# Every embedding gather of a one-core DLRM tower waits for the gather two before it

## What is computed

```python
s = jnp.sum(x, axis=-1)                        # x: (2048, 39, 64), the picked rows
z = s[:, _ROW] * s[:, _COL]                    # all pairs, (2048, 741)
h = jnp.concatenate([z, dense_ctx], axis=1)    # (2048, 757)
h = jnp.maximum(h @ W_top1 + b_top1, 0.0)      # 512 columns
h = jnp.maximum(h @ W_top2 + b_top2, 0.0)      # 256 columns
y = h @ W_top3                                 # 1 column
```

## Time and profile before

| | |
|---|---|
| median of 3 runs | 319.54 us (318.14 to 319.74) |
| profiled execution: span, first to last instruction | 314.8 us |
| PE (matmul) busy | 207.8 us, 66% |
| DVE (VectorE) busy | 144.2 us, 46% |
| ACT (ScalarE) busy | 81.2 us, 26% |
| POOL (GpSimd) busy | 114.8 us, 36% |
| the chain that ended last: PE, "issue" | 51%, 31% |

### The profile page before, as it was taken

The page is one execution under the profiler, slowest core; times in us unless marked ns, Lnnn a source line. Parts: engine busy times, 40 slices in busy tenths (PEclk is TensorE's granted clock), DMA queues, the critical chain, the costliest instruction groups (busy, mean ns, idle before and its releaser), DMA issues.

```text
span 314.8 us, 4373 instructions
## 1 busy us (share of the span) xinstructions
PE 207.8 (66%) x1659; PEld 126.9 (40%) x1659; DVE 144.2 (46%) x384; ACT 81.2 (26%) x144; POOL 114.8 (36%) x124
## 2 busy tenths in 40 slices
PE   0652102499794321118956988856999999999996
PEld 0310000344131100004613655653566776667784
DVE  2000000157990000002964679561589988968440
ACT  0200010268980000000064224210132424035432
POOL 6777777000077777740473320537310000000000
PEclk9955555589667555555985999977599999999999
DMA  7811131189924132115693676999124029100000
GB/s 290 286 29 30 27 93 25 46 300 413 418 87 129 25 69 89 25 21 186 221 342 121 217 254 218 350 351 244 25 60 150 2 77 275 52 2 2 2 0 0
DMA packets 13557, 43.70 MB, mean 139 GB/s; under 512 B 3216, under 2 KB 4256, under 8 KB 13408
## 3 DMA queue, kind: packets, MB, share of 16 engines
q1 hardware_dynamic: 9392, 39.42, 36.1%
q0 software_dynamic: 3712, 3.81, 5.8%
q10 hardware_dynamic: 432, 0.19, 0.2%
HBM read 43.14 MB, written 0.27 MB: 138 GB/s over the span
## 4 chain that ended last, share of the span: by engine, by line
PE 51%; issue 31%; DVE 7%; ACT 5%; another core or an unknown queue 3%; DMA 2%; ACTq 0%; DVEq 0%
PE g L1119 8%; PE ph L1226 8%; PE ph L1227 7%; PE ph L1230 6%; PE ph L1119 5%; PE s L1205 3%; DVE mid_sums L505 2%; PE g L1165 2%; PE g L1102 2%; PE ph L1246 2%; PE g L1140 2%; DMA stage<-early 2%; PE ph L1250 2%; PE ph L1247 2%
## 5 line engine op out<-in xcount | busy, mean ns | idle before, releaser
L429 POOL DMA_INDIRECT rows<-tab,idc x68 | 65.8, 968 | 77.9 <-DVE w_lo L522 32.8
L438 POOL DMA_INDIRECT rows<-tab,idc x48 | 46.4, 968 | 36.7 <-DVE bsum L587 18.4
L1119 PE MATMUL g<-stage,fc 128*32 128x100 f32 x378 | 27.3, 318 | 41.2 <-issue 40.2
L1119 PE MATMUL ph<-stage,fc 128*32 128x96 f32 (+2 forms) x378 | 20.9, 285 | 39.9 <-issue 30.6
L1226 PE MATMUL ph<-z_hi,w_hi 126*128 126x512 f32 (+1 forms) x96 | 44.8, 467 | 0.0
L536 DVE TENSOR_SCALAR hots<-hots,fc 125x2048 bf16<-125x2048 bf16 x28 | 20.7, 751 | 43.6 <-issue 42.5
L1227 PE MATMUL ph<-z_hi,w_lo 126*128 126x512 f32 (+1 forms) x96 | 39.7, 413 | 0.7 <-issue 0.7
L1230 PE MATMUL ph<-z_lo,w_hi 126*128 126x512 f32 (+1 forms) x96 | 39.3, 409 | 0.0
L1119 PEld LDWEIGHTS g<-stage,fc 128*32 128x32 f32 x378 | 15.8, 139 | 52.6 <-issue 50.9
L1119 PEld LDWEIGHTS ph<-stage,fc 128*32 128x32 f32 x378 | 12.4, 134 | 49.1 <-issue 47.9
L478 DVE CAST mparts<-g 125x100 bf16<-125x100 f32 x3 | 0.8, 262 | 62.4 <-PE g L1119 50.4
(11 more groups left out here) (88 smaller groups left out, 269.0 us busy)
## 6 DMA issues: line engine op xcount, KB each, us to landing
stage<-middle SPq DMA_DIRECT2D x17, 800.0 KB
hots<-shelf_scratch SPq DMA_DIRECT2D x17, 512.0 KB
stage<-early SPq DMA_DIRECT2D x3, 768.0 KB
stage<-middle SPq DMA_DIRECT2D x3, 750.0 KB
stage<-early SPq DMA_DIRECT2D x3, 640.0 KB
rows<-tab,idc POOLq DMA_INDIRECT x116
slot_b<-slot_scratch SPq DMA_DIRECT2D x8, 224.0 KB
stage<-early SPq DMA_DIRECT2D x3, 512.0 KB
```

Source lines behind the costliest of these rows:

```text
L429: pool.indirect_dma_start(rows[:, n % ROW_RING, i, :], None, gathered[i], bass.IndirectOffsetOnAxis(ap=idc[:, n, i:i + 1], axis=0)).then_i ...
L438: pool.indirect_dma_start(rows[:, n % ROW_RING, i, :], None, gathered[i], bass.IndirectOffsetOnAxis(ap=idc[:, n, i:i + 1], axis=0)).then_i ...
L1119: mm = pe.matmul(bank[j * LANE:(j + 1) * LANE, 0:w], band, stage[:, q, (r * 4 + j) * w:(r * 4 + j + 1) * w], start=(x == 0), stop=(x == PA ...
```

## The change

Two semaphores per ring slot and group take the place of one. The j-th gather of a tile signals number j mod 2. Before a gather is issued, GpSimd waits until the last gather but one has landed: in the same tile through the count of that semaphore, for the first two gathers of a tile through the tile (or group) ahead of it. So at most two gathers are on the way at any time. The order of the gathers, their number and size stay. VectorE's sums wait for both semaphores of their tile. There are 114 added waits on GpSimd, one in front of every gather but the first two.

```diff
-        rows_a_in = [sem(f"rows_a_in{t}") for t in range(ROW_RING)]
-        rows_b_in = [sem(f"rows_b_in{t}") for t in range(ROW_RING)]
+        rows_a_in = [[sem(f"rows_a_in{t}_{x}") for x in range(2)] for t in range(ROW_RING)]
+        rows_b_in = [[sem(f"rows_b_in{t}_{x}") for x in range(2)] for t in range(ROW_RING)]
...
+        def rows_a(c, x):
+            return 16 * sum((NA - SUMMED[k] + 1 - x) // 2 for k in range(c % 2, c + 1, 2))
...
+            def group_ahead_landed(c, t, kind, j):
+                n = c * TILES + t
+                if t:
+                    of, n = kind, n - 1
+                elif kind == "b":
+                    of, n = "a", n + TILES - 1
+                else:
+                    of, c, n = "b", c - 1, n - 1
+                slot = n % ROW_RING
+                if of == "a":
+                    x = (NA - SUMMED[c] - 2 + j) % 2
+                    pool.wait_ge(rows_a_in[slot][x], rows_a(c, x))
+                else:
+                    x = (NB - 2 + j) % 2
+                    pool.wait_ge(rows_b_in[slot][x], rows_b(c, x))
...
-                for i in range(SUMMED[c], NA):
-                    pool.indirect_dma_start(rows[:, n % ROW_RING, i, :], None, gathered[i],
+                for j in range(NA - SUMMED[c]):
+                    i = SUMMED[c] + j
+                    if j >= 2:
+                        pool.wait_ge(rows_a_in[slot][j % 2], rows_a(c - 2, j % 2) + 16 * (j // 2))
+                    elif n:
+                        group_ahead_landed(c, t, "a", j)
+                    pool.indirect_dma_start(rows[:, slot, i, :], None, gathered[i],
                                             bass.IndirectOffsetOnAxis(ap=idc[:, n, i:i + 1], axis=0)
-                                            ).then_inc(rows_a_in[n % ROW_RING], 16)
+                                            ).then_inc(rows_a_in[slot][j % 2], 16)
...
-                dve.wait_ge(rows_a_in[slot], rows_a(c))
+                for x in range(2):
+                    dve.wait_ge(rows_a_in[slot][x], rows_a(c, x))
```

More of the change, by code:

```diff
@@ L263, in mid_loads, with rows_b @@
             return 16 * sum(1 + (SUMMED[x] > 4) for x in range(2, c + 1))
[L265 to L269, removed]
+        def rows_a(c, x):
+            return 16 * sum((NA - SUMMED[k] + 1 - x) // 2 for k in range(c % 2, c + 1, 2))
+        def rows_b(c, x):
+            return 16 * ((NB + 1 - x) // 2) * (c // 2 + 1)
         def selects(c, which):
@@ L427, in fetch_a @@
                     pool.wait_ge(a_summed, n - ROW_RING + 1)
-                for i in range(SUMMED[c], NA):
-                    pool.indirect_dma_start(rows[:, n % ROW_RING, i, :], None, gathered[i],
+                for j in range(NA - SUMMED[c]):
[5 more added lines that the diff above has]
+                    pool.indirect_dma_start(rows[:, slot, i, :], None, gathered[i],
                                             bass.IndirectOffsetOnAxis(ap=idc[:, n, i:i + 1], axis=0)
-                                            ).then_inc(rows_a_in[n % ROW_RING], 16)
+                                            ).then_inc(rows_a_in[slot][j % 2], 16)
             def fetch_b(c, t):
                 n = c * TILES + t
+                slot = n % ROW_RING
                 if c >= 2:
                     pool.wait_ge(b_summed, n - ROW_RING + 1)
-                for i in range(NA, NL):
-                    pool.indirect_dma_start(rows[:, n % ROW_RING, i, :], None, gathered[i],
+                for j in range(NB):
+                    i = NA + j
+                    if j >= 2:
+                        pool.wait_ge(rows_b_in[slot][j % 2], rows_b(c - 2, j % 2) + 16 * (j // 2))
+                    else:
+                        group_ahead_landed(c, t, "b", j)
+                    pool.indirect_dma_start(rows[:, slot, i, :], None, gathered[i],
                                             bass.IndirectOffsetOnAxis(ap=idc[:, n, i:i + 1], axis=0)
-                                            ).then_inc(rows_b_in[n % ROW_RING], 16)
+                                            ).then_inc(rows_b_in[slot][j % 2], 16)
             pool.memset(tparts[:, :, :], 0.0)
@@ L585, in sum_b @@
                 slot = (c * TILES + t) % ROW_RING
-                dve.wait_ge(rows_b_in[slot], rows_b(c))
+                for x in range(2):
+                    dve.wait_ge(rows_b_in[slot][x], rows_b(c, x))
                 dve.tensor_reduce(bsum[:, t, 0:NB], rows[:, slot, NA:, :], AX.X, ALU.add).then_inc(b_summed, 1)
```

## The result

| | before | after |
|---|---|---|
| median of 3 runs each | 319.54 us (318.14 to 319.74) | 270.79 us (270.01 to 272.56) |
| span of the profiled execution | 314.8 us | 269.0 us |
| last gather starts at, and from there to the end | 228.91, 85.9 us | 243.59, 25.4 us |

The change made the kernel faster: ratio 0.850, 95% interval 0.845 to 0.854. I had forecast 325 us. The direction was wrong; the time lies where rival 1 put it.

What follows compares the result with a forecast made beforehand. TensorE standing during gather runs (94 of 314.8 us), then matmuls in the last stretch, bound the kernel. 5.6 + 2.5 - 2.5 + 0.4 = 6.0 us more, later runs 0: span 320.8, plus 4.7, predicted 325 us; range 319 to 347.

Steps and rivals of the forecast that it cites:

- rival 1: Slower gathers end TensorE's standing and then bound the kernel: 262 us, 237 to 314, chance 0.38.
- main step: Waits are already met in mid run, so gathers stay 1.25 us apart and TensorE's slow pace inside runs stays.
- The wait in mid run: GpSimd's wait without loads: landing 2.14 us against a look at 2.2 us, so met and free; far end 6 us per run.
- The stall: TensorE nearly stands during long gather runs and a few us behind: two slow stretches, 94 of 314.8 us, taken to stay.
- a tenth less pace is enough: Argument for rival 1: leftover about 0.11 us per gather, 9% of the 1.25 us pace, so slightly slower gathers free TensorE.
- picture of a pile that forms: Rival 1's mechanism: 40 gathers pile something up; if landing signals queue behind it, the new wait keeps it from forming.
- Delay beside loads: Gathers wait beside table loads: third gather 3.0 us late; 5.6 us in the first run, 2.5 us in the second.
- Rows are needed late: Later gather runs: last sum comes 61 us behind the last gather's start, so their 5 to 20 us delay counted 0.
- Rival 1's sum: Gather-bound time: 116 gathers at 1.3 us, 151; 36 beside loads, 54 more; 4 start, 25 end, 5 around: 239 us.
- rival 1's signs: "Issue" below 15% of the chain, first slow stretch's 30 matmuls done by 25 us, GpSimd busy nearly to the end.
- Rivals 2 and 3: 2: waits met, delay given back, 319.5 us, chance 0.16. 3: late landing signals lengthen TensorE's standing, 340 us, chance 0.06.
- the slow case: The outcome that the change makes the kernel slower, chance 0.43; the forecast's own range was 0 to 28 us more.

Runs made afterwards that it cites:

- the copy with the stall: The kernel before, unchanged, run and traced again on another chip: 318.12 us against 318.32, ratio 0.996; 17% "issue" in its chain.
- the bound of three: At most three gathers on the way, added to the kernel before: 235.76 us, ratio 1.191, measured only without the stall.
- the slower memset: A GpSimd memset of 128x512 in front of each gather of the kernel before, no landing waits: 235.51 us, ratio 1.195, without the stall.
- at most 4: Kernel before with at most four gathers on the way: 299.49 us (ratio 0.950) with the stall, 213.10 us (1.077) without.
- memset 256: Kernel before with a 128x256 GpSimd memset before each gather, no landing waits: 276.91 us against 317.43 with the stall; 214.79 us (1.086) without.

## Why the prediction was wrong

**The step that failed** is the one the forecast rested on, "whether waiting gathers still make TensorE stand". I took it that they do, because I held that in mid run the wait is already met and the pace stays. I had written: "I am wrong in the main step if TensorE's pace inside a run of gathers changes". It did, from 30 matmuls to 287 in 39 us. The measured time lies within the 236 to 338 us that I gave over all cases only because that range takes in rival 1; the forecast's own 319 to 347 us misses it, and that the wide range holds is no merit of the forecast.

**The wait in mid run.** I set the landing (2.14 us, from the packets of the earlier trace rows) against the time at which GpSimd looks (2.2 us) and called the wait met. The packets are not the signal. Without loads beside it, the profile gives 2.5 us from issue to landing, and the trace after has a gather at 186.02 that was held by the one at 182.78, 3.24 us before it. A margin of 0.06 us was not enough to build the main case on. The pace there is 1.50 us; my pairs were to take 2.5 us, with 2.8 us at the far end, and take 3.0.

The Trainium skill ("DMA: Bandwidth & Descriptors", section on the anatomy of a GpSimd DMA) gives about 2.0 us for setup and completion plus the bytes, by estimate 2.1 us for such a gather. Completion is counted in it, so its like is the landing by the signal, 2.5 us, which is 0.4 us above; that the packets end after 2.14 us was no agreement, as I had taken it. Under loads 5.1 to 5.7 us were measured.

**The stall.** It goes because the gathers are thinned out, in mid run and beside loads: shown with the stall by three kernels, two of which thin them out in mid run (270.79 and 276.91 us) and one of which does not (299.49). Rival 1 had it that slower gathers free TensorE, but its "a tenth less pace is enough" is not what was seen: with a seventh less (1.25 to 1.45 us) half of the stall is left, and it is nearly gone only with the bound of two, whose gathers are 2.08 us apart on the mean. Its picture of a pile that forms was not tested. A rest is still there in that kernel too. In the trace after, behind a gather run 1.5 us apart, TensorE works in slots again (65.38, 66.14, 66.88), until it has its full rate back at 67.63 us:

```profile
65.38 0.41 PE L1149 MATMUL g<-stage,fc 128*32 128x100 f32 x6 [0.35 <-issue]
66.14 0.38 PE L1149 MATMUL g<-stage,fc 128*32 128x100 f32 x4 [0.35 <-issue]
66.88 0.41 PE L1149 MATMUL g<-stage,fc 128*32 128x100 f32 x6 [0.36 <-issue]
67.63 1.27 PE L1149 MATMUL g<-stage,fc 128*32 128x100 f32 x48 [0.35 <-issue]
```

I had lowered that rival's chance a little for the rule of the Trainium skill ("SBUF — State Buffer", "Who interferes with whom") that a DMA never contends with a compute engine. Without the stall the traces agree with it (452 matmuls beside 31 gathers); with the stall TensorE's rate falls and rises with how densely the gathers come, whatever the path is by which it does. The rule was no reason against the rival.

**Delay beside loads.** The third gather was to start near 9.9 us and started at 10.45, held 3.83 us: that part was right. Its sum was not. I had 5.6 us for the first run and 2.5 us for the second, and called the rest covered. The first run ends at 89.49 us instead of near 59. I had counted only the load bursts that the stalled trace shows; once TensorE is free, loads run at 259 GB/s in the same stretch instead of 40 and meet the gathers all along. "Rows are needed late" was true of a kernel whose rows came at 1.25 us; at 2.08 us VectorE waits 67.7 us for them.

**Rival 1's sum.** 205 us of gathers (151 + 54), 4 before, 25 behind, 5 around: 239, and weighted 262. Measured: 239.3 us of gathers (243.59 - 4.28), 4.3, 25.4, and 1.8 around the span make 270.8. The form was right, the gather term 34 us short: 1.3 us for a gather alone is 1.50, and more than the 36 I counted meet loads; 68 waited for a landing.

**The rivals.** Of rival 1's signs, "issue" at 11% came in (I asked for below 15, a narrow mark beside the 17% of the copy with the stall); so did the matmuls of the first slow stretch (103 had passed by 56 us before, 268 by 25 us after) and GpSimd at work to 243.59 of 269.0 us. Rivals 2 and 3 are out in this comparison. That the slow case could be the one to hold elsewhere, at 38%, I had not foreseen: my range was on top of a stall that I took for a property of the kernel. One sentence touched the other case, "if the stall were not there, a delay of 5.6 us would be paid by these idles and cost nothing". Without the stall the change costs 74 us (271.75 - 197.64). A reason to doubt it stood in the earlier trace rows: waits of 50 us whose releaser issues one matmul in 2.80 us "for nothing that the profile shows". What no row explains may not be there the next time.

**Still open.** What sets the condition, and by what path gathers then hold TensorE up; the kernel with a met wait in front of every gather where the stall is present (it was measured four times, each time without it); the bound of three and the slower memset with the stall; and which of number on the way or spacing counts. For a version better than the kernel before in both conditions there is no candidate: at a price of 15 us without the stall (at most 4) 18 us are won with it, and at 17 us (memset 256) 41.

## What to carry to other kernels

A stall that the profile can't put to any releaser is to be measured more than once, on more than one chip, before a change is judged by it; here the sign of the result hangs on it. A bound on how many gathers are on the way sets their pace to about the landing time over the bound, and where loads run the landing time to use is the one beside them (5 to 6 us), not the one without (2.5 us). Even without loads it came out longer than that: a pair took 3.0 us under the bound of two, not 2.5. Where gathers bound the end, it does not matter whether a wait or idle work thins them out: count pace times number, and add what follows the last.

## What the runs showed of the hardware

- The same program takes 198 or 318 us, and the runs of one comparison agree on one of them; it is not tied to the chip (chip 8: 197.64 and 317.43 us).
- In the slower condition TensorE's small matmuls beside a run of gathers go in steps of 0.70 to 0.73 us: down to one per 2.80 us with gathers 1.25 us apart, and mostly four to six per step, at times at full rate, at 1.45 to 1.50 us.
- A gather of 32 KB lands 2.5 us behind its issue without loads beside it and 5.1 to 5.7 us beside table loads (medians). A wait in front of a gather that is already met showed no cost over 116 gathers (ratios 0.995 and 1.013, both intervals around 1).
- The granted clock followed TensorE's work: 0.50 (1.2 GHz) in the slow stretch of the earlier trace rows, a mean of 0.67 in the same stretch after, and 0.87 in the met-wait kernel without the stall. It did not set the pace: at 0.50 TensorE passed 25 small matmuls in 1.28 us.
